# A fused interaction-network kernel: which tiles GpSimd, VectorE and TensorE's full-precision path take, and how many product slots there are

## What is computed

```python
x0 = xk = e                                   # [1024, 39, 16], gathered rows
for idx, (W, b) in enumerate(params):         # three layers, 128 outputs each
    z = relu(einsum('bhd,bkd,hks->bsd', x0, xk, W) + b)
    if idx != 2:
        xk = z[:, :64, :]                     # feeds the next layer
        direct.append(z[:, 64:, :])
    else:
        direct.append(z)
logit = sum(concatenate(direct, axis=1), axis=-1)
h = relu(concatenate([logit, dense_ctx], 1) @ W_top1 + b_top1)
h = relu(h @ W_top2 + b_top2)
y = h @ W_top3
```

## Time and profile before

| engine | busy us | share of the span |
|---|---|---|
| TensorE, matmuls | 1182.3 | 95% |
| TensorE, weight loads | 726.7 | 58% |
| VectorE | 1055.4 | 84% |
| ScalarE | 580.3 | 46% |
| GpSimd | 1015.9 | 81% |

### The profile page before, as it was taken

The page is one execution under the profiler, slowest core; times in us unless marked ns, Lnnn a source line. Parts: engine busy times, 40 slices in busy tenths (PEclk is TensorE's granted clock), DMA queues, the critical chain, the costliest instruction groups (busy, mean ns, idle before and its releaser), DMA issues.

```text
span 1250.1 us, 14867 instructions
## 1 busy us (share of the span) xinstructions
PE 1182.3 (95%) x3856; PEld 726.7 (58%) x3856; DVE 1055.4 (84%) x919; ACT 580.3 (46%) x563; POOL 1015.9 (81%) x637
## 2 busy tenths in 40 slices
PE   0389999999999999999999999999999999999898
PEld 0155656656565665656566665656566565656565
DVE  2278998989899898989899898989989898999782
ACT  1145454544445444454544444454545444454453
POOL 6778898988888898888889798888989888756661
PEclk9999999999999999999999999999999999999999
DMA  4785626274563627356461635556262745625000
GB/s 124 250 269 187 220 62 224 99 217 164 171 210 99 215 78 236 137 171 210 132 227 60 211 135 186 195 164 217 66 217 101 215 166 171 210 97 165 1 1 1
DMA packets 110269, 196.21 MB, mean 157 GB/s; under 512 B 52975, under 2 KB 64334, under 8 KB 110249
## 3 DMA queue, kind: packets, MB, share of 16 engines
q1 hardware_dynamic: 100009, 193.33, 46.8%
q0 software_dynamic: 10240, 2.64, 1.9%
HBM read 193.36 MB, written 12.78 MB: 165 GB/s over the span
## 4 chain that ended last, share of the span: by engine, by line
PE 67%; POOL 16%; issue 7%; DVE 5%; ACT 3%; DMA 1%; POOLq 0%; DVEq 0%; SPq 0%; ACTq 0%
PE acc L850 65%; POOL lo L465 9%; POOL emb L455 7%; DVE prod L729 2%; ACT hi L588 2%; DVE lo L742 2%; DVE acc L729 1%; DVE hi L739 0%; DMA x_tiles<-x_rows 0%; POOL pairs_r L480 0%; DMA x_rows<-x_rows 0%; PE acc L928 0%; DMA x_rows<-emb 0%; DMA emb<-table,block_idx 0%; DMA base_sb<-base 0%
## 5 line engine op out<-in xcount | busy, mean ns | idle before, releaser
L729 DVE TENSOR_TENSOR prod<-x_tiles,xk 128x1024 f32<-128x1024 f32 (+2 forms) x643 | 757.5, 1215 | 129.6 <-PE acc L850 87.0
L465 POOL TENSOR_TENSOR lo<-prod,hi 128x1024 fp32r<-128x1024 f32 (+1 forms) x288 | 688.8, 2394 | 135.4 <-ACT hi L588 130.6
L850 PE MATMUL acc<-prod,wfull 128*128 128x512 f32 (+2 forms) x1408 | 660.7, 593 | 0.0
L588 ACT ACTIVATE hi<-prod 128x1024 fp32r<-128x1024 f32 (+1 forms) x291 | 308.1, 1060 | 399.6 <-DVE prod L729 316.2
L850 PE MATMUL acc<-hi,whi 128*128 128x512 f32 (+1 forms) x800 | 353.8, 442 | 58.9 <-ACT hi L588 58.9
L850 PEld LDWEIGHTS acc<-prod,wfull 128*128 128x128 f32 (+2 forms) x1408 | 266.4, 189 | 206.0 <-issue 177.7
L455 POOL DMA_INDIRECT emb<-table,block_idx x320 | 308.8, 965 | 69.2 <-issue 62.0
L850 PE MATMUL acc<-lo,whi 128*128 128x512 f32 (+1 forms) x736 | 316.4, 517 | 6.6 <-POOL lo L465 5.4
L850 PE MATMUL acc<-hi,wlo 128*128 128x512 f32 (+1 forms) x800 | 316.5, 396 | 0.0
L850 PEld LDWEIGHTS acc<-lo,whi 128*128 128x128 f32 (+1 forms) x736 | 137.9, 189 | 138.6 <-issue 103.3
L850 PEld LDWEIGHTS acc<-hi,whi 128*128 128x128 f32 (+1 forms) x800 | 151.4, 189 | 114.2 <-issue 70.6
(11 more groups left out here) (73 smaller groups left out, 171.9 us busy)
## 6 DMA issues: line engine op xcount, KB each, us to landing
x_tiles<-x_rows SPq DMA_DIRECT2D x304, 512.0 KB, 5.0
x_rows<-x_rows SPq DMA_DIRECT2D x16, 624.0 KB
x_tiles<-x_rows SPq DMA_DIRECT2D x32, 256.0 KB, 5.6
x_stack<-x_rows SPq DMA_DIRECT2D x48, 156.0 KB
emb<-table,block_idx POOLq DMA_INDIRECT x320, 3.7
x_rows<-emb SPq DMA_DIRECT2D x16, 152.0 KB, 3.3
x_tiles<-w SPq DMA_DIRECT2D x1, 768.0 KB, 6.4
x_tiles<-w SPq DMA_DIRECT2D x1, 704.0 KB, 9.5
```

The source lines that it names most:

```text
L465: nc.gpsimd.tensor_tensor(lo[0:r, product_slot(j), :], prod[0:r, product_slot(j), :], hi[0:r, part_slot(j), :].bitcast(f32), ALU.subtract) ...
L588: nc.scalar.activation(hi[0:r, part_slot(j), :], held(n, parity, j)[0:r, :], ACT.Copy).then_inc(hi_ready, 1)
L729: nc.vector.tensor_tensor(held(n, parity, j)[0:r, :], in0, in1, ALU.mult).then_inc(product_ready, 1)
L850: mm = nc.tensor.matmul(z[:, c], w[0:r], part[0:r, c], start=first and i == 0, stop=last and i == len(weights) - 1)
```

## The change

Three of the G tiles of L1 and L2 become D tiles, the order of kinds within the two layers is rewritten, and there are eight product slots for six. G has then the indices 0, 3, 6, 10, 13, 16 in L1 (6 tiles) and 0, 3, 5, 7, 10, 13, 16 in L2 (7 tiles); D has 2, 5, 8, 15, 18 in L1 and 9, 15, 18 in L2. A block has 15 tiles of G, 8 of D, 2 of H and 22 of F; each layer has as many F tiles as before. `Z_TOP1`, from which the last block's L2 takes in the top network, is 6 for 7. The host orders the weights by kind, as it did.

```diff
-Z_TOP1 = 7
+Z_TOP1 = 6
...
-KINDS = ["GFFGFFF", "GFDGF" * 2 + "GFHGF" + "GFDGF", "GFFGF" + "GFFGD" + "GFHGF" + "GFDGF"]
+KINDS = ["GFFGFFF", "GFDGFDGFDFGFHGFDGFDF", "GFFGFGFGFDGFHGFDGFDF"]
...
-PRODS, PARTS = 6, 4
+PRODS, PARTS = 8, 4
```

## The result

The changed kernel takes 1296.55 us (median of five, 1294.47 to 1297.45), the kernel before 1252.46 us beside it: a ratio of 1.0348, with a 95% interval of 1.0334 to 1.0363. It is slower by 44 us. The forecast was 1283, from 1273 to 1308. The profiled execution took 1297.45 us, 1295.6 of them from first to last instruction.

The account below looks back on a forecast made before the run. TensorE was taken as the bound, at its rate in all but 0.2 us of a 71.95 us block. The profiled 1251.9 + 30.8 (L2's gathers) - 1 (last block) = 1281.7, or 1283.0 in median terms; range 1273 to 1308.

Parts of the forecast that it names:

- What bounds the kernel: TensorE at its rate in all but 0.2 us of a block; GpSimd late only at L2's tile 10, 0.33 us.
- Part 1: Matmuls in every layer: as many as before, so the pure 71.8 us a block stay.
- Part 4: L2's gathers as 2, 3, 3: TensorE waits 2.53 us at tile 7, +2.2 us a block, +30.8 in 14 blocks.
- not-slower rival: GpSimd's stretch isn't tied to L1's end and starts 2.5 us earlier, so no stall: 1247.6 us, chance 0.08.
- The clock: TensorE's granted clock behind the 14 stalls in L2: taken not to fall, 0 us.
- a rival for it: Clock falls behind some or all of L2's 14 stalls: 1307 us if in all, 1295 if in half; chance 0.22.
- main case: The L2 stall as worked out, without a fall of the clock: 1274 to 1290 us, likeliest 1283; chance 0.65.
- signs that the prediction named for being wrong: A period below 72, TensorE waiting for `hi` or VectorE's lo, or matmuls 0.43 us apart behind each stall.
- Part 2: Three subtractions move from GpSimd (7.2 us a block less) to VectorE (3.4 more), whose lead covers them: 0.
- Part 3: Two more product slots: F products run further ahead, GpSimd's stretch doesn't start earlier: 0.
- Part 5: Last block: 1.3 us gained at index 8, the 3.0 us stall moves elsewhere; together -1, from -4 to +3.
- VectorE rival: VectorE becomes the bound through waits at its eight D tiles a block: 1318 us, chance 0.05.

Follow-up runs that it names:

- sixteen: The changed kernel with L1's last D tile back as G and gathers dealt 9 in L1, 4 in L0, 7 in L2 behind four G tiles: 1244.82 us.
- spread4: The changed kernel with L2's gathers behind four G tiles again, as 2, 2, 2, 2 for 2, 3, 3: 1255.73 us, 1.0027 of the kernel before.
- old_three: The kernel before with only L2's gathers laid behind three G tiles, as 2, 3, 3: 1270.15 us, ratio 1.0141.
- l2_alone: The kernel before with the new kinds in L2 only, and eight slots: 1292.96 us, ratio 1.0327.
- slots6: The changed kernel with six product slots for eight: 1314.55 us, ratio 1.0492.
- sub18_first: The changed kernel with VectorE's subtraction of L1's tile 18 moved ahead of the sum over direct2 and L0's first product: 1296.59 us, ratio 1.0346.
- l1_alone: The kernel before with the new kinds in L1 only, and eight slots: 1255.41 us, ratio 1.0028.
- gathers_moved: The changed kernel with tile 18's subtraction ahead of the sum and gathers dealt 10 in L1, 4 in L0, 6 in L2: 1250.22 us, ratio 0.9982.

## Why the prediction was right, point by point

- **What bounds the kernel.** TensorE at its own rate, with one late place in L2. Shown: `sixteen`, which removes the waits, gains 0.35 us a block and no more.
- **Part 1** stands: TensorE's matmuls are as many, L0 takes 11.38 us for 11.36.
- **Part 4, the gathers,** carried the forecast and is confirmed in its number and its place: a stall worked out as 2.53 us and measured as 2.46; +2.2 us a block against 2.19; 30.8 us in 14 blocks against 30.7. `spread4` and `old_three` show the cause from both sides, the latter with 1270.15 us for an expected 1268.5. The start of GpSimd's stretch is tied to L1's end at 3.53 us in both kernels, which was what the not-slower rival denied. The old wait at tile 10 costs some 0.1 us more than the 0.33 that I read: L2 takes 30.66 us with it and 30.23 in block 14, where there is none. A wait at tile 7 carries the same extra, so the difference comes out right.
- **The clock** is where most of the 13.5 us between forecast and result went. I had weighed 1.7 and 3.0 us of idleness, taken no fall for the stall between them, and kept a rival for it, at 0.22, with 1295 us if the clock fell in half the blocks. That rival came nearest, and the result lies outside the main case, 1274 to 1290; the range holds it only because it was drawn to hold the clock too. It fell in 6 of 14 blocks, 9 us. That 1295 is so near is in part luck: the rival had 12 us for seven falls, and the waits for VectorE, which it didn't have, made up for the rest. Two of the signs that the prediction named for being wrong are in the trace, the matmuls 0.43 us apart behind a stall and TensorE waiting for VectorE's lo. The nearest row, the one at 3.0, had pointed there, and I set it aside as one case. It was no rule either, as `l2_alone` shows with 3.0 us and no fall. A term between zero and all would have been the better guess for a stall that lies between the two rows.
- **Part 2, VectorE,** has the step that failed. I put tile 18's subtraction one product behind its product, at the end of L1, ahead of L0. By `tiles`, which runs over all three layers in one loop, it is two products behind, behind the sum as well. Its price was 0.41 us in each of 14 blocks and 1.6 in block 0, some 7 us, where I had put 0. VectorE's lead at L0's start is 4.7 us (701.55 against 706.24) for the 5 worked out, but that confirms nothing: TensorE waits for VectorE just before, and in `slots6` the lead is 4.7 us as well. At L1's start I had up to eight tiles, some 12 us; it is 6.9, and VectorE then idles 0.9 us at tile 3 until TensorE has freed a slot and 1.0 us for ScalarE's rounding of tile 2 (its timeline at 673.04 and 676.43). The rounding that I had bounded, tile 18's, isn't what it waits for. That `sub18_first` doesn't bring the 7 us back shows only that GpSimd's stretch stands behind this wait; `l1_alone`, where GpSimd isn't late by as much, has the whole 0.4 us a block.
- **Part 3, the slots,** was right that they don't move the stall, and that they are worth nothing in the old steady state. It was wrong that they are worth 0 here: they give VectorE its lead into L1 and are worth 18 us in the changed kernel, and 4 in the kernel before, in its last block.
- **Part 5, the last block:** -3.1 us for -1, inside its range. As expected the 3.0 us stall moved. It appears in two places, as 2.6 us for ScalarE's `hi` of tile 13 and 2.6 for VectorE's lo of tile 15, which stands behind the split of the dense inputs. `old_slots8`, the old kinds with eight slots, gains 5.1 us in the same stretch (129.3), and `slots6`, the new kinds with six, 1.6 (132.8). So, by one trace each, either alone gains there, the slots more, and the gains don't add up.
- **The VectorE rival** (1318 us) didn't come: in `gathers_moved`, with all eight D tiles, a block takes 71.93 us.

The clock's falls at 2.3 us speak against the Trainium skill (TensorE: Matmul & The Clock Gate, section Why this matters for your kernels), which puts the danger at idle gaps over about 3 us. The measurement decides: 2.3 us was enough in 6 of 14 blocks here and in 9 of 14 in `l2_alone`, whose 3.0 us in the last block were not. Why a given block is hit and the next, with the same stall, isn't, stays open; no run was made for it.

## What to carry to other kernels

A change of what an engine computes can change where its other duties fall: here a count of tiles fed a formula that dealt DMA issues, and three subtractions fewer made GpSimd late. Look for everything that is worked out from the list you edit, and lay the engine's timeline against its consumer's from the last event that ties both, tile by tile; the busy share of either says nothing about it. Relief ahead of such an event is lost as idleness.

## What was not expected of the hardware

- TensorE's granted clock fell behind stalls of 2.3 to 2.6 us in some blocks and not in others: 5 to 9 of 14. At 1.1 and 1.4 us it never fell, at 3.6 it always did. Behind 3.0 us in the last block it fell in the kernel before, in `old_three` and in `old_slots8`, and not in `l2_alone`.
- A fall cost some 1.5 us a block behind 2.3 us, and 2.75 behind 3.6, where the clock was 0.56 over 6.7 us. How long it stays down isn't given by the stall alone: behind 3.0 us the clock was 0.53 over 3.5 us in the kernel before, and 0.50 over 6.0 us in `old_three`.
